# Row maxima of the last graph layer: scores gathered alone from a small table, maxima kept by group and scanned by blocks at the end

## The reference, cut to what matters

```python
xt = x @ W
s_node = xt @ a_src
d_node = xt @ a_dst
e_contrib = edge_attr @ a_edge
e_all = concatenate([e_contrib, e_contrib, zeros])
logits = leaky_relu(s_node[src] + d_node[dst] + e_all, 0.2)
m = segment_max(logits, dst)
z = exp(logits - m[dst])
att = z / segment_sum(z, dst)[dst]
out = segment_sum(att[:, None] * xt[src], dst)
```

## Time and profile before

| | |
|---|---|
| median of 3 runs | 18622.1 us (18571.03 to 18630.84) |
| span of the profiled execution, first to last instruction | 15897.9 us |
| time of the profiled execution itself | not given; only its span is |
| median less the span | 2724.2 us |
| rows stage, about | 12165 to 13248 us |
| maxima stage, about | 13258 to 14382 us |
| sums stage, about | 14406 to 15787 us |

### The profile page before, as it was taken

How to read it: one execution, slowest core, us unless ns; L and a number is a source line. 1 busy time by engine, 2 the same in 40 slices (tenths; PEclk the granted TensorE clock), 3 DMA queues, 4 the chain that set the end, 5 groups by cost and what they waited for, 6 DMA issues and landing times. The chain is left out here.

```text
span 15897.9 us, 333194 instructions
## 1 busy us (share of the span) xinstructions
PE 10323.3 (65%) x72558; PEld 8007.5 (50%) x72559; DVE 10176.4 (64%) x36116; ACT 4490.5 (28%) x11901; POOL 9058.2 (57%) x10038
## 2 busy tenths in 40 slices
PE   6555555555537777776965665646676775667886
PEld 5333333333326666665864444433345664336886
DVE  9666666666643444446866776772375666888887
ACT  0111111111101333332113440006401223556885
POOL 0477777777754777767764445547501445554442
PEclk9777777777765777775555667765555665558998
DMA  9722222222242444453318997757663887885664
GB/s 369 308 80 80 80 80 81 82 80 80 80 84 68 79 80 79 80 72 81 67 36 208 327 325 237 224 169 258 225 205 112 269 268 250 267 266 203 210 213 157
DMA packets 2144345, 2589.93 MB, mean 163 GB/s; under 512 B 892241, under 2 KB 1761818, under 8 KB 2144194
## 3 DMA queue, kind: packets, MB, share of 16 engines
q1 hardware_dynamic: 1749158, 1741.66, 37.9%
q0 software_dynamic: 353792, 655.17, 13.1%
q10 hardware_dynamic: 41244, 191.56, 3.1%
HBM read 1738.44 MB, written 848.86 MB: 163 GB/s over the span
## 5 line engine op out<-in xcount | busy, mean ns | idle before, releaser
L566 POOL DMA_INDIRECT edges_by_dst<-rec,pos x1568 | 1538.8, 981 | 1030.7 <-DVE rec L501 558.3
L989 POOL DMA_INDIRECT sc_rows<-src_table,sc_idx x1664 | 1595.0, 959 | 607.4 <-issue 496.8
L566 POOL DMA_INDIRECT edges_by_cell<-rec,pos x1568 | 1546.3, 986 | 514.7 <-issue 500.1
L1757 PE MATMUL ex_rows<-table,ex_oh 128*128 x6528 | 1138.7, 342 | 747.9 <-DVE ex_stage L1733 315.7
L642 PE MATMUL xps<-ident,ea 128*128 128x128 f32 x784 | 216.6, 432 | 1744.1 <-DMA ea<-in_edge_attr_dram 1744.1
L1845 PE MATMUL gs_part<-gs_rows,gs_oh 128*128 128x192 bf16 x6528 | 1009.1, 317 | 517.6 <-DVE gs_oh L1818 350.6
L1757 PEld LDWEIGHTS ex_rows<-table,ex_oh 128*128 128x128 bf16 x6528 | 736.9, 130 | 1149.3 <-issue 1109.3
L2225 ACT ACTIVATE key_in_block<-at_rows,first_node 128x66 f32<-128x66 f32 x4352 | 1083.7, 336 | 269.2 <-PE at_part L2253 248.7
L2253 PE MATMUL at_part<-cell_edge_term,key_in_block 128*66 128x128 f32 x8704 | 1066.3, 287 | 115.6 <-issue 96.4
L530 DVE SCALAR_TENSOR_TENSOR junk<-rowb,keycol,earlier 128x128 f32<-128x128 f32 (+1 forms) x3136 | 1123.6, 413 | 1.2
L1845 PEld LDWEIGHTS gs_part<-gs_rows,gs_oh 128*128 128x128 bf16 x6528 | 691.1, 130 | 835.7 <-issue 396.7
(11 more groups left out here) (402 smaller groups left out, 27305.6 us busy)
## 6 DMA issues: line engine op xcount, KB each, us to landing
ex_keys<-src_key_rows SPq DMA_DIRECT2D x1632, 128.0 KB, 4.1
gs_rows<-dst_rows_by_src SPq DMA_DIRECT2D x1088, 192.0 KB
rowb<-sort_key_rows SPq DMA_DIRECT2D x392, 512.0 KB, 5.1
ex_keys<-dst_key_rows SPq DMA_DIRECT2D x1088, 128.0 KB
dst_rows_by_src<-patY ACTq DMA_DIRECT2D x1, 104448.0 KB, 417.2
rows_by_src<-ex_stage SPq DMA_DIRECT2D x544, 192.0 KB
scored_dst_rows_by_src<-patZ ACTq DMA_DIRECT2D x1, 71808.0 KB, 637.1
scored_rows_by_src<-ex_stage SPq DMA_DIRECT2D x544, 132.0 KB
```

Of the source, the lines that this page charges most:

```text
L566: nc.gpsimd.indirect_dma_start(out=out, out_offset=bass.IndirectOffsetOnAxis(ap=pos[:, u, k, j:j + 1], axis=0), in_=row, in_offset=None).t ...
L989: nc.gpsimd.indirect_dma_start(out=rows[:, u, j, :], out_offset=None, in_=tabS, in_offset=bass.IndirectOffsetOnAxis(ap=idx[:, u, j:j + 1], ...
L1757: m = nc.tensor.matmul(rows[k][u % deep][r // 2][:, r % 2, 0:W], oh[k][:, u % deep, r * P:(r + 1) * P], t3[:, bass.ds(held[k][u], 1), :].r ...
```

## The change

- **Rows stage.** The stored k = 1 row loses its last two columns (4 x 64 numbers, 1024 bytes); its scores go to a plane of `own_terms`, and after the last group SP stores that plane, 544 x 4 numbers per partition, to a new table `scores_by_src` in one DMA. The scattered rows have 4 x 65 numbers, the scores last.
- **Maxima stage.** Work comes in turns of 4 quads. POOL gathers 16 bytes per chunk from the small table, straight into `edge_scores`; SP loads the other scores, 16 groups at once. The split into three parts moves from POOL (four small instructions per quad) to ScalarE and VectorE (two each per turn). The 8 column updates per quad and the register loads are gone; the results of the reductions are copied by ScalarE into a plain table `group_tops` (L2079 of the new file). The selection matrices `pick` are made earlier, on POOL during a `sum_rows` of the layer before. The loop body holds 8 quads.
- **New stage** `block_maxima` ("mb"), after it: a running maximum over the groups of a block by a scan, and the last group of each block is picked out by transposes and matmuls.
- **Sums stage.** The exponential is written into the messages' last column, in two instructions per quad, the rows are 64 wide, and the messages have 8 places instead of 4.

```diff
+                                 stage[1][:, u, :]).then_inc(s_out[1][u].sem, 16)
                 skewed(sp, n, [(4, load), (-1, store)])
+                wait(sp, s_ev[1], D.NG)
+                sp.dma_start(XS[0:D.NCH, :].rearrange("(g p) r -> p g r", p=P), dn[:, 1, :, :]).then_inc(s_sc.sem, 16)
                 for k in range(2):
                     for u in range(RING):
                         wait(sp, s_out[k][u], n * 16)
+                wait(sp, s_sc, 16)
...
-                    nc.vector.tensor_copy(stage[0][:, u, :, 0:C], of[:, :, 0:C])
-                    nc.vector.tensor_tensor(stage[0][:, u, :, C], of[:, :, C], K.ecA[:, bass.ds(g, 1), :].rearrange("p o r -> p (o r)"), ALU.add)
+                    nc.vector.tensor_copy(stage[0][:, u, 0:SLOTS * C].rearrange("p (r c) -> p r c", c=C), of[:, :, 0:C])
+                    nc.vector.tensor_tensor(stage[0][:, u, SLOTS * C:SLOTS * (C + 1)], of[:, :, C], K.ecA[:, bass.ds(g, 1), :].rearrange("p o r -> p (o r)"), ALU.add)
                     nc.vector.tensor_copy(dn[:, 0, bass.ds(g, 1), :].rearrange("p o r -> p (o r)"), of[:, :, C + 1]).then_inc(s_ev[0].sem, 1)
...
-                    nc.scalar.copy(stage[1][:, u, :, 0:C + 1], of[:, :, 0:C + 1])
-                    nc.scalar.copy(dn[:, 1, bass.ds(g, 1), :].rearrange("p o r -> p (o r)"), of[:, :, C + 1]).then_inc(s_ev[1].sem, 1)
+                    nc.scalar.copy(stage[1][:, u, :].rearrange("p (r c) -> p r c", c=C), of[:, :, 0:C])
+                    nc.scalar.copy(dn[:, 1:3, bass.ds(g, 1), :].rearrange("p s o r -> p s (o r)"), of[:, :, C:C + 2].rearrange("p r s -> p s r")).then_inc(s_ev[1].sem, 1)
...
+                def load_scores(i, u):
+                    if u % RING == 0:
+                        t = i * 2 + u // RING
+                        w = u // RING
+                        wait(sp, s_g, t - 1)
+                        sp.dma_start(score[:, 1, bass.ds(t * TURN, TURN), :], view[:, bass.ds(t * TURN, TURN), SLOTS * C:SLOTS * (C + 1)]).then_inc(s_in[1][w].sem, 16)
...
-                skewed(sp, n, [(1, load)])
+                skewed(sp, n // 2, [(2 * RING, load_scores), (1, load)], ring=2 * RING)
...
+                for t in range(n):
+                    wait(pool, s_g, t - 1)
...
+                    for v in range(TURN):
+                        g = t * TURN + v
+                        nc.gpsimd.indirect_dma_start(out=score[:, 0, g, :], out_offset=None, in_=XS,
+                                                     in_offset=bass.IndirectOffsetOnAxis(ap=K.cfrom[:, g:g + 1], axis=0)).then_inc(s_in[0][t % 2].sem, 16)
...
+                def first_parts(i, u):
+                    if u % RING == 0:
+                        t = i * 2 + u // RING
+                        wait(act, s_g, t + 1)
+                        wait(act, s_t, (t - 1) * RING)
+                        nc.scalar.copy(parts_of(u // RING, 0), of_turn(t)).then_inc(s_first.sem, 1)
+
+                def second_parts(i, u):
+                    if u % RING == 0:
+                        t = i * 2 + u // RING
+                        wait(act, s_r, t + 1)
+                        nc.scalar.copy(parts_of(u // RING, 1), rest[:, :, :, :]).then_inc(s_second.sem, 1)
...
-                skewed(act, n, [(1, copy_turned), (1, keep), (1, penalties)])
...
+                skewed(act, n // 2, [(RING, first_parts), (RING - 1, second_parts), (1, copy_turned), (1, penalties), (-1, keep)], ring=2 * RING)
...
                 def scores(i, u):
-                    q = i * RING + u
+                    if u % RING == 0:
+                        t = i * 2 + u // RING
+                        w = u // RING
+                        wait(dve, s_in[0][w], (i + 1) * 16 * TURN)
+                        wait(dve, s_in[1][w], (i + 1) * 16)
+                        own = score[:, 0, bass.ds(t * TURN, TURN), :]
+                        nc.vector.tensor_tensor(own, own, K.ecA[:, bass.ds(t * TURN, TURN), :], ALU.add).then_inc(s_g.sem, 1)
+
+                def first_rest(i, u):
+                    if u % RING == 0:
+                        t = i * 2 + u // RING
+                        wait(dve, s_first, t + 1)
+                        wait(dve, s_gp, t)
+                        nc.vector.tensor_tensor(rest[:, :, :, :], of_turn(t), parts_of(u // RING, 0), ALU.subtract).then_inc(s_r.sem, 1)
+
+                def second_rest(i, u):
+                    if u % RING == 0:
+                        t = i * 2 + u // RING
+                        wait(dve, s_second, t + 1)
+                        nc.vector.tensor_tensor(parts_of(u // RING, 2), rest[:, :, :, :], parts_of(u // RING, 1), ALU.subtract).then_inc(s_gp.sem, 1)
+
+                def maxima(i, u):
+                    q = i * 2 * RING + u
...
-                                                           accum_out=gm[:, w, e:e + 1]).then_inc(s_max.sem, 1)
-                    wait(dve, s_max, (q + 1) * 2 * QUAD)
...
-                            nc.vector.tensor_tensor(top[:, bass.ds(b, 1)], top[:, bass.ds(b, 1)], gm[:, w, e:e + 1], ALU.max).then_inc(s_top.sem, 1)
...
-                    for k in range(2):
-                        held[k] = nc.values_load_multi_w_load_instructions(K.cblk[0:1, k, bass.ds(i * RING * QUAD, RING * QUAD)], engines=DVE_ONLY,
...
-                skewed(dve, n, [(2, scores), (0, maxima)], blocks)
+                                                           accum_out=found[:, w, k, v:v + 1]).then_inc(s_max.sem, 1)
+                skewed(dve, n // 2, [(RING, scores), (0, maxima), (RING - 1, first_rest), (RING - 2, second_rest)], ring=2 * RING)
...
+                step(nc.vector.tensor_tensor(pen[:, :, 1:NG], K.cfirst[:, :, 1:NG], K.cfirst[:, :, 0:NG - 1], ALU.is_gt))
+                step(nc.vector.tensor_single_scalar(pen[:, :, 1:NG], pen[:, :, 1:NG], -BIG, ALU.mult))
+                for k in range(2):
+                    nc.vector.tensor_tensor_scan(top[:, k, :], pen[:, k, 0:NG], gm[:, k, :], -BIG, ALU.add, ALU.max)
+                step(nc.vector.tensor_single_scalar(last[:, :, :], pen[:, :, 1:NG + 1], 0.0, ALU.is_lt))
+                step(nc.vector.scalar_tensor_tensor(last[:, :, :], K.cfirst[:, :, :], 1.0, last[:, :, :], ALU.add, ALU.mult))
+                step(nc.vector.tensor_single_scalar(last[:, :, :], last[:, :, :], -1.0, ALU.add))
+                for q, (k, c, w) in enumerate(chunks):
+                    wait(dve, s_t, q + 1)
+                    nc.vector.tensor_copy(topT[0:w, k, q % nch, :], tp[q % 2][0:w, 0, :])
+                    nc.vector.tensor_scalar(pick[0:w, k, q % nch, :], K.iota[0:w, 0:NB], tp[q % 2][0:w, 1, 0:1], None, ALU.is_equal).then_inc(s_c.sem, 1)
+                wait(dve, s_f, 1)
+                step(nc.vector.tensor_scalar(none[:, :, :], some[:, :, :], -1.0, FAR, ALU.add, ALU.mult))
+                nc.vector.tensor_tensor(tops[:, :, :], found[:, :, :], none[:, :, :], ALU.add)
...
+                for q, (k, c, w) in enumerate(chunks):
+                    wait(pe, s_c, q - 1)
+                    nc.tensor.transpose(tp[q % 2][0:w, 0, :], top[:, k, c:c + w], K.ident[:, :])
+                    nc.tensor.transpose(tp[q % 2][0:w, 1, :], last[:, k, c:c + w], K.ident[:, :]).then_inc(s_t.sem, 1)
+                wait(pe, s_c, len(chunks))
+                for k in range(2):
+                    for to, lhs in ((found, None), (some, K.ones)):
+                        for q in range(nch):
+                            w = chunks[q][2]
+                            m = nc.tensor.matmul(to[:, k, :], topT[0:w, k, q, :] if lhs is None else lhs[0:w, :], pick[0:w, k, q, :],
+                                                 start=q == 0, stop=q == nch - 1)
+                m.then_inc(s_f.sem, 1)
...
-                def weights(i, u):
-                    q = i * RING + u
-                    wait(act, s_a, q + 1)
-                    wait(act, s_msg, (q - 1) * E)
-                    nc.scalar.activation(z[:, u % 2, :, :, :], arg[:, u % 2, :, :, :], ACT.Exp).then_inc(s_z.sem, 1)
-
-                def messages(i, u):
-                    q = i * RING + u
-                    wait(act, s_z, q + 1)
-                    for k in range(2):
+                def weights(k):
+                    def run(i, u):
+                        q = i * RING + u
+                        wait(act, s_a, q + 1)
+                        wait(act, s_mm, (q - 1) * E + (k + 1) * QUAD)
+                        nc.scalar.activation(msg[:, k * QUAD:(k + 1) * QUAD, :, C], arg[:, u % 2, k, :, :], ACT.Exp).then_inc(s_z.sem, 1)
+                    return run
+
+                def messages(first, end):
+                    def run(i, u):
+                        q = i * RING + u
+                        k = first // QUAD
+                        wait(act, s_z, 2 * q + k + 1)
                         wait(act, s_in[k][u % 2], (i * (RING // 2) + u // 2 + 1) * 16 * (QUAD if k == 0 else 1))
-                    for e in range(E):
-                        k, v = e // QUAD, e % QUAD
```

(16 more changed lines are left out.)

231 lines of the change are left out of this document (106 added, 125 removed).

## The result

The changed kernel takes 18,836 us (median of 4 runs, 18,794 to 18,848), the kernel before 18,613 on the same chip: ratio 1.0123, 95% interval 1.0107 to 1.0138. The forecast was 18,431, range 18,270 to 18,590.

A forecast was written before the change was run, and what follows sets the result against it. It took DMA traffic to bound the rows stage, VectorE the maxima, and waits for products to hold both VectorE and ScalarE in the sums. Terms -253 - 1 + 50 - 13 + 27 - 1 + 0 = -191 us gave 18,431 us, range 18,270 to 18,590.

The forecast's parts named there:

- The baseline: Whole kernel: the 2,724 us between profiled span (15,897.9) and median (18,622.1) taken as unchanged, all terms inside the span.
- The maxima loop: Maxima stage: dropping updates, picking and register loads makes a four-quad turn 24.3 us, 34 turns 826 us; -253 us.
- the first stall: Maxima loop: ScalarE's copy waits for a VectorE subtraction and delays the next quad's penalties; VectorE idle about 2.6 us per turn.
- the second: Maxima loop: TensorE turns the next turn's first tile ahead of spreading step 3; 0.9 us of idle per turn.
- POOL needs 0.96 + 0.30 us per gather, 16 of them 20.2 us per turn, under 24.3: Maxima loop: check that POOL's gathers, 20.2 us per turn, would not be late against a 24.3 us turn.
- POOL becomes the bound: Rival, maxima stage: gathers take 1.66 us with issue, 26.6 us per turn, +78 us, kernel 18,522; 10%.
- The small table: After the rows stage: SP's store of 69,632 runs of 16 bytes takes 60.5 us, about 10 hidden; +50 us.
- the start of the maxima: Before the first reduction: early selection matrices help, but 32 gathers must come first, 43 us against 44.0; -1 us.
- The sums stage: Sums stage: added exponential is covered by ScalarE's waiting, eight message places gain nothing; 0, bounds -50 and +29 us.
- VectorE adds the products in the same order: Sums stage: reason given for 0 us, that VectorE's work and order stay although eight places let ScalarE run ahead.
- The new stage: Between maxima and sums: scans, passes, transposes and small matmuls +27 us, the dropped copy of the first `tops` -1.
- The rows stage: Rows stage: DMAs move 1.15% less of 1,080 us per group; -13 us, bounds 0 and -58.

The follow-up runs named there:

- e7: Changed kernel with ScalarE's messages again tied to the product four back, as with four message places: 19,077 us, ratio 1.0238 to the kernel before.
- e8: Kernel before with only the sums-stage part: eight message places and weights written by ScalarE into the messages' last column; ratio 0.9889.
- e9: Changed kernel with the small table stored by partition, in runs of 8,704 bytes instead of 16: 18,792 us, ratio 1.0088 to the kernel before.
- e14: Kernel before with POOL pauses ahead of each two scatters in the sort and each two gathers in the score stage: 17,799 us, ratio 0.9651.
- e13: Changed kernel with only a 1 us POOL clearing ahead of each two gathers of the maxima: ratio 0.9881 to the kernel before.
- e15: Changed kernel with table by partition, VectorE's subtraction moved earlier, and POOL pauses in maxima, sort and score stage: 17,436 us, ratio 0.9456 to before.

## Why the prediction was wrong

**The baseline.** The step "the 2,724 us between them I take as unchanged" failed first. Less than 2 us lay outside the span (18,579.2 against 18,577.5). The shown execution was an unusual one, without "remote" stalls beside POOL's DMAs, and I summed its terms onto the median of others. A span 15% under the run time was the sign, and I passed over it. What made that execution so different no run shows.

**The maxima loop, -253, measured +301.** The terms were nearly right for a loop without gathers: 26.2 us per turn for 24.3, the first stall 4.8 for 2.6 (it missed the copy behind the second penalty), the second 1.0 for 0.9. The step that failed is "POOL needs 0.96 + 0.30 us per gather, 16 of them 20.2 us per turn, under 24.3". I took the gathers to cost POOL's time alone. They cost VectorE's too once they run unbroken for some 4 us, and that added 498 us. Before, a quad's four gathers lasted 5 us, then POOL spent over 2 us on splitting scores (L2033 to L2039), and VectorE lost 19.6 us to "remote" in the whole stage. None of my rivals had it; "POOL becomes the bound" named the right engine with the wrong mechanism (a gather took 0.94 us, not 1.36).

**The small table, +50, measured +87** with the start of the maxima. The mechanism was right, and the measured cost lies inside its bounds of 35 to 212; the size was scaled from a load by bytes, and a store of such runs took 2.3 times a load's time per run.

**The sums stage, 0, measured -196.** I had bounded it at -50, half of VectorE's waits of the shown profile. The eight places brought it (e7, e8). How they do so is read from the waits and not tested by itself: in the usual execution TensorE loses time beside the gathers, four places pass each such pause on to ScalarE and back, and eight take it up. The argument "VectorE adds the products in the same order" is true and didn't bound anything, for VectorE waited 370 us for products there instead of 105.

**The rest.** The new stage is +25 for +26. The rows stage is +20 for -13, and it isn't noise alone: the old one took 1,214 us (e8) where the new one took 1,242 and 1,243 on the same chip (e7, e9), and 1,203 (e14) against 1,224 and 1,214 (e13, e15). So this term had the wrong sign, by 10 to 30 us; what makes the new rows stage longer no run shows.

## What to carry to other kernels

Set the profiled span beside the run times before anything else; if they differ by more than the runs among themselves, the trace shows an execution unlike the timed ones, and its waits aren't those that you will be timed on. Look in it for engines that stand still with all inputs ready beside long unbroken rows of POOL's indirect DMAs, and try a pause of 0.5 to 1 us ahead of each two of them before touching anything else: here that alone was worth 3.5% in two stages and 2.4% in a third. The pauses come out of POOL's time, so they pay only while the stalls cost more. A change that batches such DMAs can lose more by that than it saves in instructions. And a store of 16-byte runs that a stage waits for is dear: here 88 us went when it was turned so that a partition writes in one piece.

## What the runs showed of the hardware

- Beside unbroken indirect DMAs of POOL, VectorE and TensorE (and, by the waits put down to "remote", ScalarE) stood still with nothing to wait for that the trace shows, 0.5 to 6.3 us at a time in the stretches above, from 3 to 6 us after the first of them; sixteen in a row cost a turn of VectorE 14.6 us ((1,390 - 892) / 34). Sixteen clearings by POOL of 952 ns each cost nothing (893 us), and clearings put between the gathers took the stall away (907, 897 us). The Trainium skill ("SBUF — State Buffer", Who interferes with whom) tells of VectorE and GpSimd blocking each other over a shared pair of ports, says that a VectorE instruction with at most one SBUF input outside the two-port modes doesn't contend, and that TensorE and ScalarE never wait. The reductions here have one input in SBUF and one in PSUM, and the products above are TensorE's: by that rule TensorE, and VectorE if its reductions run outside those modes, should not have stopped, and both did. That the engines lacked instructions rather than data would fit single products 0.7 us apart, but late loads of instructions are not what the traces show: the queue that loads them moved 2 packets in the whole sort, in the shown profile of before as in the fresh one, and 11 in the maxima of the changed kernel against 8 without gathers. What stops the engines stays open.
- 69,632 stored runs of 16 bytes took 103 us from issue to the next stage, 23.7 ns per run and DMA engine, at 12 GB/s; as one run of 8,704 bytes per partition the same stretch took 16 us.
- Of two profiled executions of the kernel before, the one without "remote" waits had a span of 15,898 us, the other one, with 7,357 us of them over all engines, 18,578 us.
